# One token tile ahead in the first stage of a perceiver kernel, its last keys in one transfer of 88 rows, its phase rows padded to 128

## What is computed

```
x = x + L0_xattn(layernorm(x), ctx)   # q = x Wq + bq, k = c Wk + bk, v = c Wv + bv over all 1601 context rows
                                      # softmax(q k^T / sqrt(256)) v
x = x + L0_mamba(layernorm(x))        # in_proj, conv over 4 tokens, selective scan, out_proj
x = x + L0_ffn(layernorm(x))
x = x + L1_xattn(layernorm(x), ctx)   # 16 heads; the mask leaves context rows 0 to 63
x = x + L1_attn(layernorm(x))         # attention in which two phases per token come in through Wtq and Wfq
x = x + L1_experts(layernorm(x))      # 8 experts, the best 2 of each token
```

## Time and profile before

| | us |
|---|---|
| median of 3 runs | 666.38 (666.16 to 670.92) |
| the profiled execution | 666.37 |
| its span, first to last instruction | 664.6 |
| TensorE busy | 603.7 (91%) |
| VectorE busy | 463.7 (70%) |
| ScalarE busy | 367.9 (55%) |
| GpSimd busy | 234.0 (35%) |
| HBM read | 83.50 MB, 127 GB/s over the span |

### The profile page before, as it was taken

How to read it: one execution, slowest core, us unless ns; L and a number is a source line. 1 busy time by engine, 2 the same in 40 slices (tenths; PEclk the granted TensorE clock), 3 DMA queues, 4 the chain that set the end, 5 groups by cost and what they waited for, 6 DMA issues and landing times. The chain is left out here.

```text
span 664.6 us, 11620 instructions
## 1 busy us (share of the span) xinstructions
PE 603.7 (91%) x4390; PEld 456.9 (69%) x4390; DVE 463.7 (70%) x790; ACT 367.9 (55%) x694; POOL 234.0 (35%) x187
## 2 busy tenths in 40 slices
PE   4999998999998877878788999999999899999997
PEld 4455554454356766767677888887777678889897
DVE  3743333346867999999999517788977868876554
ACT  1311111124988999999999333344656455556343
POOL 2000000000069999999898200025641012231000
PEclk9999999999999999999999999999999989999999
DMA  9999999994912222233320000000100022210000
GB/s 319 399 401 392 392 391 391 394 322 141 268 61 97 95 99 110 99 107 111 113 96 1 1 0 18 1 0 18 36 2 2 2 64 80 64 48 1 33 1 32
DMA packets 31294, 86.47 MB, mean 130 GB/s; under 512 B 8076, under 2 KB 19816, under 8 KB 29064
## 3 DMA queue, kind: packets, MB, share of 16 engines
q1 hardware_dynamic: 31096, 85.67, 36.0%
q10 hardware_dynamic: 144, 0.06, 0.1%
HBM read 83.50 MB, written 1.11 MB: 127 GB/s over the span
## 5 line engine op out<-in xcount | busy, mean ns | idle before, releaser
L761 POOL TENSOR_TENSOR dbu<-du,bs 128x1024 f32<-128x1024 f32 x64 | 149.7, 2368 | 6.7 <-DVE w_in L1009 4.7
L890 ACT ACTIVATE weighed<-T,CT 128x256 f32<-128x256 f32 x222 | 95.0, 593 | 1.3 <-PE T L1088 0.9
L1009 DVE TENSOR_TENSOR_SCAN w_in<-hS,dbu 128x1024 f32<-128x1024 f32 x42 | 94.6, 2271 | 0.4 <-ACT hS L879 0.4
L879 ACT ACTIVATE hS<-delta,negA 128x504 f32<-128x504 f32 x128 | 90.8, 814 | 4.9 <-DVE xn L1009 2.2
L1102 PE MATMUL Y<-ident,weighed 128*128 128x128 f32 x512 | 66.7, 273 | 0.0
L1088 PE MATMUL T<-ident,w_in 128*128 128x128 f32 x336 | 45.9, 279 | 19.8 <-ACT weighed L890 14.3
L1102 PEld LDWEIGHTS Y<-ident,weighed 128*128 128x128 f32 x512 | 57.9, 141 | 0.5
L1088 PEld LDWEIGHTS T<-ident,w_in 128*128 128x128 f32 x336 | 36.0, 140 | 30.7 <-DVE w_in L1009 27.4
L383 POOL COPY w_xp<-w_xp 128x64 f32<-128x64 f32 x3 | 0.6, 234 | 145.6 <-DMA w_out<-in_w_out 145.6
L1009 DVE TENSOR_TENSOR_SCAN xn<-hS,dbu 128x1024 f32<-128x1024 f32 x22 | 50.0, 2274 | 2.3 <-ACT hS L879 2.3
L297 PE MATMUL O<-cN,pT 128*64 128x256 f32 x384 | 46.7, 385 | 5.3 <-DMA cN<-in_ctx 5.3
(11 more groups left out here) (426 smaller groups left out, 1351.3 us busy)
## 6 DMA issues: line engine op xcount, KB each, us to landing
cT<-in_ctxT SPq DMA_DIRECT2D x8, 3202.0 KB, 22.0
cN<-in_ctx SPq DMA_DIRECT2D x8, 3072.0 KB, 24.4
bs<-b_rows SPq DMA_DIRECT2D x32, 512.0 KB, 3.6
raw_w<-in_w SPq DMA_DIRECT2D x16, 256.0 KB, 2.9
w<-in_w SPq DMA_DIRECT2D x7, 256.0 KB, 7.7
vs<-vx SPq DMA_DIRECT2D x8, 136.0 KB, 2.4
x<-in_x SPq DMA_DIRECT2D x2, 512.0 KB, 5.2
cR<-in_ctx SPq DMA_DIRECT2D x8, 128.0 KB
```

Source lines behind the costliest of these rows:

```text
L761: e.tensor_tensor(dbu[s % NB][:, :, :], half(m.du, s // DS), row, ALU.mult).then_inc(s_bu, 1)
L879: i = e.activation(by_batch(A[s % 2][:, j * HALF:(j + 1) * HALF]), by_batch(m.delta[:, c, h * HALF:(h + 1) * HALF]), ACT.Exp, scale=m.negA ...
L890: i = e.activation(weighed[s % 2][:, q * Q:(q + 1) * Q], T[:, q * Q:(q + 1) * Q], ACT.Copy, scale=c_of(s, q))
L1009: e.tensor_tensor_scan(S[s % NS], A[s % 2][:, :], dbu[s % NB][:, :, :].rearrange("p c n -> p (c n)"), 0.0, ALU.mult, ALU.add).then_inc(s_h, 1)
```

## The change

The work is the same except for the placing of some keys and rows of zeros. Its parts are:

- **Start.** The block of its own and its barrier are gone. Tokens are loaded in three parts (tile 0, tiles 1 to 3, 4 to 7), `cT` of tile 0 in two parts (columns 0 to 1023 and 1024 to 1600), in between. Projection is done in five groups of tiles (0, 1, 2-3, 4-5, 6-7), and the scores of tile 0 begin when tile 0 alone is projected. `turn(0)` and two of the projections change places. ScalarE and VectorE share the moves to `qkT`. TensorE first runs 22 transposes of the identity (`keep_busy`). Two masks on VectorE come later.
- **Last keys.** `cR` holds the last 88 keys on 88 partitions, loaded by one transfer. The chunks of `cN` use 127 (chunk 0) or 126 partitions. `cN` itself is loaded as before, so 23 keys a batch are loaded twice.
- **Phases.** `reT` and `wfq` are 128 rows, zero beyond the five; GpSimd sets the zeros.

The diff, cut to its core:

```diff
-REST = LK - MAIN
+REST = 88
+CUT = LK - REST
...
-def load_columns(e, k, i, r):
-    e.dma_start(k.cT[r][:, :, :, :], k.ctxT[2 * i:2 * i + 2].rearrange("b (c p) n -> p b c n", p=P)
-                ).then_inc(k.s_dT[r], 16)
+def load_columns(e, k, i, r, at=slice(0, LK), done=None):
+    e.dma_start(k.cT[r][:, :, :, at], k.ctxT[2 * i:2 * i + 2, :, at].rearrange("b (c p) n -> p b c n", p=P)
+                ).then_inc(done or k.s_dT[r], 16)
...
-    for rows in (slice(0, 64), slice(64, REST)):
-        e.dma_start(k.cR[r][rows, :, :], k.ctx[2 * i:2 * i + 2, MAIN + rows.start:MAIN + rows.stop, :].rearrange("b p d -> p b d")
-                    ).then_inc(k.s_dR[r], 16)
+    e.dma_start(k.cR[r][:, :, :], k.ctx[2 * i:2 * i + 2, CUT:LK, :].rearrange("b p d -> p b d")).then_inc(k.s_dR[r], 16)
 
 
 NORMED = (range(0, 4), range(4, 7), range(7, 8))
+FIRST = (range(0, 1), range(1, 4), range(4, TILES))
+GROUPS = (range(0, 1), range(1, 2), range(2, 4), range(4, 6), range(6, TILES))
...
-            return slice(c, c + (P - 1) * ROWS + 1, ROWS) if c < ROWS else slice(MAIN, LK)
+            return slice(c, c + (P - 2) * ROWS + 1, ROWS) if c < ROWS else slice(CUT, LK)
+
+        def n_turned(c):
+            return P - 1 if c < ROWS else REST
 
         def n_keys(c):
-            return P if c < ROWS else REST
+            return len(range(c, CUT, ROWS)) if c < ROWS else REST
...
+            def keep_busy(n):
+
+                for i in range(n):
+                    e.transpose(X[:, i % 4 * P:(i % 4 + 1) * P], k.ident[:, :], k.ident[:, :])
...
+                if i == 0 and chunks[0] == 0:
+                    e.wait_ge(k.s_d0, 16)
+                else:
+                    e.wait_ge(s_dT[r], 16 * (i // 2 + 1))
...
-            turn_first(0)
-            e.wait_ge(k.s_w0, k.n_w0)
+            def pair(a, b, n):
+                return [a[:, 0:n], b[:, 0:n]]
+
+            def side(a, n):
+                return [a[:, 0:n], a[:, n:2 * n]]
+
+            e.wait_ge(k.s_const, 2)
+            keep_busy(22)
+            turn_query_weights()
+            fold_query_bias()
+            turn_tokens(0, bank[3])
             fold()
-            project(0)
-            e.wait_ge(s_pe, 2)
-            scores(0)
-            project(1)
-            e.wait_ge(s_q0, 2)
-            e.wait_ge(s_pe, 4)
+            project(0, pair(bank[0], bank[1], P))
+            fold_key_bias()
+            e.wait_ge(s_qa, 1)
+            e.wait_ge(s_qd, 1)
+            scores(0, range(0, 2))
+            turn_tokens(1, bank[3][:, D:2 * D])
+            turn_tokens(2, O)
+            e.wait_ge(s_e0, 2)
+            scores(0, range(2, 4))
+            project(1, side(tps[1], P))
+            project(2, side(tps[0], 2 * P))
+            turn_tokens(3, O)
+            e.wait_ge(s_qa, 3)
+            turn_tokens(4, tps[1])
+            e.wait_ge(s_ex, 1)
+            e.wait_ge(s_qd, 3)
+            turn(0, 0)
+            project(3, side(bank[0], 2 * P))
+            project(4, side(bank[1], 2 * P))
+            turn(0, 1)
+            e.wait_ge(s_qa, 5)
+            e.wait_ge(s_qd, 5)
             for i in range(1, TILES + 2):
-                if i <= TILES:
+                if 1 < i <= TILES:
...
-            done(e.activation(k.reT[:, 0:HALF], T[0][0:5, :], ACT.Copy), "reT")
+            done(e.activation(k.reT[0:5, 0:HALF], T[0][0:5, :], ACT.Copy), "reT")
+            e.memset(k.reT[:, 0:HALF], 0.0)
...
-                done(e.activation(reT[:, HALF:TOK], BK[RE][0:5, :], ACT.Copy), "reT")
+                done(e.activation(reT[0:5, HALF:TOK], BK[RE][0:5, :], ACT.Copy), "reT")
+            e.memset(reT[:, HALF:TOK], 0.0)
...
-        k.wfq = sb("wfq", [5, D])
+        k.wfq = sb("wfq", [P, D])
...
+            e.wait_ge(k.s_wz, 1)
...
+        def first_loads(e):
+            tiles = t["x"].rearrange("b l d -> (b l) d").rearrange("(t p) d -> p t d", p=P)
+
+            def load_tokens(f):
+                ts = slice(FIRST[f][0], FIRST[f][-1] + 1)
+                e.dma_start(k.x[:, ts, :], tiles[:, ts, :]).then_inc(k.s_x[f], 16)
+
+            load_tokens(0)
+            for n, w in (("wq0", k.wq0), ("wk0T", k.wk0T)):
+                e.dma_start(w[:, :, :], t[n].rearrange("(c p) n -> p c n", p=P)).then_inc(k.s_w0, 16)
+            load_columns(e, k, 0, 0, slice(0, 2 * HALF), k.s_d0)
+            load_tokens(1)
+            load_columns(e, k, 0, 0, slice(2 * HALF, LK))
+            load_tokens(2)
+            load_columns(e, k, 1, 1)
+            load_vectors(e, 0, 1, k.s_bv)
...
+            e.memset(k.wfq[:, :], 0.0).then_inc(k.s_wz, 1)
...
-        k.reT = k.rows[0:5, 0:4, :].rearrange("p r d -> p (r d)")
+        k.reT = k.rows[:, 0:4, :].rearrange("p r d -> p (r d)")
```

More of the change, by code:

```diff
@@ L468, in _, with statistics @@
         def _(e):
-            for half in range(2):
-                ts = range(4 * half, 4 * half + 4)
+            def statistics(f):
+                ts = FIRST[f]
                 hs = slice(ts[0], ts[-1] + 1)
-                e.wait_ge(k.s_x[half], 16)
+                e.wait_ge(k.s_x[f], 16)
                 for t in ts:
```

273 lines of the change are left out of this document (146 added, 127 removed).

## The result

The changed kernel took 670.65 us (median of 20 runs, 667.38 to 672.95) beside 667.38 us for the kernel before (20 runs, 665.41 to 670.92): a ratio of 1.0045, 95% interval 1.0033 to 1.0058, so it is 3.0 us slower. The forecast was 5.3 us faster, and the time lies 3.7 us above the upper end of its range. The profiled execution took 671.38 us, its span 669.6 us.

The account below looks back on a forecast made before the run. The prediction took transfers to set the first stage's pace, with TensorE waiting. From 666.37 us, last keys -3.0, start +0.3 and phases -2.6 summed to -5.3, giving 661.1 us; range 656.3 to 667.

Parts of the forecast that it names:

- What bounds the kernel now: First stage: transfers set the pace and TensorE waits for `cN` once a tile; its last awaited landing, at 136.18 us, sets the end.
- TensorE's part is even: First stage, chunk products: the last chunk's take the same columns and 12 chunks lose a row or two; no time was added.
- Last keys: First-stage `cR` transfer: half of the 7.46 us lost in six slow stretches goes, more bytes cost 0.7; -3.0 us.
- So the loss goes with the pair of `cR` transfers and not with the number of rows: Slow stretches: inferred from 30 to 34 us, where `wv` ran beside `cR` of tile 0 and the loss was 1.24 us.
- The bound above, +3.3: Worst case for the 88-row transfer: the stretches' loss grows with the rows, 88/65, +2.6 and +0.7 us for bytes.
- 88 rows weigh more: Rival on the slow stretches: loss grows with the rows, 3.3 us; 667.4 us with the clock held, 670.0 without; chance 0.07.
- shared out unevenly: Rival on the `cR` transfer: some engines carry twice the rows, 1.9 us in six tiles, 666.0 us in all; chance 0.05.
- The rival in which the slow stretches vanish: First-stage transfers: the whole 7.46 us loss goes, -6.8 us after the added bytes, 657.3 us in all; chance 0.24.
- Start: Kernel start: first scores at 12 to 14 us instead of 23.62, worth 0; splitting `cT` of tile 0 costs 0.3 us.
- the lead of about 10 us would count: First stage: if transfers were much faster, so that they no longer covered it, TensorE's earlier start would count; nothing was taken.
- Phases: Phase stage near 530 to 537 us: padding 5 rows with zeros keeps the full clock; -2.6 us, at worst 0.
- The sum: Whole kernel: -3.0 + 0.3 - 2.6 = -5.3 us from the profiled 666.37 us, giving 661.1 us.

## Why the prediction was wrong

- *What bounds the kernel now*: right for the kernel before, where transfers set the pace. It then took this for the changed kernel too, without working out how little TensorE had to lose: its own period of 15.04 us stood 1.7 us under the transfers' 16.7, and the edit took 1.68 of that.
- *The step that failed*: "TensorE's part is even: the last chunk's products take the same columns, and 12 chunks lose a row or two." The products with `cN` lose a row or two, but the transposes lose a column, from 128 to 127, and the load of 127 columns takes twice the time: 1.68 us a tile, 5.0 us in all when done alone. The sum has no term for it. With 128 columns the changed kernel is 1.0004 of before.
- *Last keys*, -3.0 us: wrong in sign, +2.6 us alone. It rests on "So the loss goes with the pair of `cR` transfers and not with the number of rows", read off one row, the stretch at 30 us, where `wv` was under way. `wv` came on 128 partitions, the form that turned out to be nearly harmless (370 and 393 GB/s at that place once `cR` has this form too), so the row says nothing of 88 rows. One transfer on 88 partitions left the stretches at 329 to 332 GB/s. The bound above, +3.3, held. Of the rivals, "88 rows weigh more" gave 3.3 for this part and "shared out unevenly" 1.9; 2.6 +- 0.9 does not tell them apart, and 96 and 128 rows say that neither names the mechanism. The rival in which the slow stretches vanish had 7.46 us for them; with the bytes of 128 rows (0.30 us a tile at 424 GB/s, 1.8 in six) that is 5.7 us less, and 6 us less was measured, for 128 rows and not for 88.
- *Start*, 0 with 0.3 for the split transfer: the size is right, +0.5 us (-0.5 to +1.7), and the first scores at 13.12 lie in the 12 to 14 given. The reason is only half right, and the rest is luck. The lead was to be eaten by waits for transfers several times as long; where the start stands alone these waits grew by 1.0 us, and of the lead of 10 us 1.3 are left at the scores of tile 1 (33.59 us), because the work moved behind the first scores is done there. So "the lead of about 10 us would count" if the cover went was wrong as well: in the changed kernel TensorE is the bound, and the next stage starts at 167.50 us, where it is 167.65 with 127 columns alone.
- *Phases*, -2.6 us: the mechanism was right (1.00 from 530 to 538 us, 2.46 us gained at the place), its size 1.9 us (0.5 to 3.3). The term took the fall as certain before and gone after; it stood in 7 of 8 profiles without the padding and 2 of 12 with it. Two slips in the working cost little: "0.22 us each pair of instructions" is 0.22 for each one, as 1.73 for 8 says, and the durations come from the rows of the chain, while the timeline has 2.86 us for the 12 instructions where 2.6 was worked out.
- *The sum*: 5.3 us less were forecast, 3.0 more were measured, a miss of 8.3. Taken alone, the last keys miss by 5.6 us, the columns by 5.0, the phases by 0.7 and the start by 0.2. That is 11.5, and the difference is mostly the 88 rows, which cost nothing more beneath a busy TensorE. The sum also started from 666.37 us, where the median of 20 runs is 667.38.

## What to carry to other kernels

For FP32 transposes try an even number of columns, 128 where the data allow it, even if one of the columns is not used afterwards; an edit that only "loses a row" on one operand may lose a column on another. Try a small transfer between large ones in the shape of these, here 128 partitions, even if it moves twice the bytes. Before taking an engine as slack, work out its own period beside the bound's, and what eats the difference.

## What the runs showed of the hardware

- FP32 transposes of every twelfth element with 127, 125, 123, 121, 99 and 97 columns took 365 to 423 ns a record, with 126, 124, 120, 116, 112 and 96 272 to 306, and with 49, 50 and 52 all 273; on the path it was 0.14 us each for 127 against 128.
- With 1 KB packets on 128 partitions between larger ones the engines kept 408 to 417 GB/s; with 64 + 1, 88 and 96 partitions 327 to 351 for some 6 us a tile, and the large packets slowed too (252 ns against 274 to 276).
- Padding 5 rows with zeros to 128 left a fall of the clock in 2 of 12 profiles where it was in 7 of 8; padding 8 rows, in 0 of 5 where it was in 7 of 15. Five falls stood behind waits of 2.02 to 2.82 us between products on 126 or 128 rows, and one wait of 2.19 us had none.
